# A graph network layer on one core: six of 512 gathered edge-tile pairs fetched by SyncE, and a shifted schedule

## The reference

```
ea  = edge_attr @ w_e + b_e               # 131072 x 64 by 64 x 256
msg = relu(x[src] + ea)                   # a gather of 131072 rows of x, 1 KB each
agg = segment_sum(msg, dst, 8192)
t   = x + agg
h_local = bn1(relu(t @ w1 + b1) @ w2 + b2 + x)
# attention in blocks of 32 nodes, 4 heads
q, k, v = split(x @ in_w.T + in_b)
h_attn  = bn2(softmax(q k / 8) v @ out_w.T + out_b + x)
o   = h_local + h_attn
o   = bn3(o + relu(o @ m_w1 + m_b1) @ m_w2 + m_b2)
out = layernorm(x + o)
```

## Time and profile before

| | |
|---|---|
| median of three runs | 1324.22 us (1323.06 to 1324.55) |
| the profiled execution | 1324.22 us |
| its span, first to last instruction | 1322.4 us |
| mean granted TensorE clock | 0.947 |
| instructions | 22286 |

### The profile page before, as it was taken

How to read it: one execution, slowest core, us unless ns; L and a number is a source line. 1 busy time by engine, 2 the same in 40 slices (tenths; PEclk the granted TensorE clock), 3 DMA queues, 4 the chain that set the end, 5 groups by cost and what they waited for, 6 DMA issues and landing times.

```text
span 1322.4 us, 22286 instructions
## 1 busy us (share of the span) xinstructions
PE 1174.0 (89%) x7309; PEld 664.5 (50%) x7309; DVE 823.5 (62%) x2089; ACT 548.5 (41%) x1077; POOL 971.0 (73%) x1032
## 2 busy tenths in 40 slices
PE   6787899898989898898998899889898899999987
PEld 3444454444445454454444445444454446766666
DVE  5747467667565675756667475575655757558544
ACT  1443435343434444344343434434343434444443
POOL 7777777777777777777777777777777777777760
PEclk7787999899989989899999999899898999999999
DMA  9464545555556555555555555555564555645540
GB/s 332 130 180 149 178 130 177 170 169 169 155 152 178 168 164 169 159 180 153 170 159 179 153 152 175 164 170 154 159 185 147 169 170 152 186 146 160 171 134 20
DMA packets 113268, 216.10 MB, mean 163 GB/s; under 512 B 21504, under 2 KB 62720, under 8 KB 113152
## 3 DMA queue, kind: packets, MB, share of 16 engines
q0 software_dynamic: 49152, 134.28, 34.9%
q1 hardware_dynamic: 62560, 77.09, 18.0%
q10 hardware_dynamic: 1440, 3.29, 0.6%
HBM read 197.80 MB, written 16.78 MB: 162 GB/s over the span
## 4 chain that ended last, share of the span: by engine, by line
POOL 34%; PE 27%; issue 15%; DVE 13%; DMA 5%; DVEq 4%; ACT 1%
POOL xg L369 34%; PE bank L747 16%; PE bank L777 6%; DMA xg<-in_x_dram,srcs 5%; DVE bank L592 4%; DVEq L608 3%; PE bank L792 3%; DVE mx L636 2%; DVE aggT L624 2%; DVE dif L641 2%; PE bank L801 1%; PE bank L874 1%; DVE o L668 1%; PE bank L848 1%; DVE probT L657 1%
## 5 line engine op out<-in xcount | busy, mean ns | idle before, releaser
L369 POOL DMA_INDIRECT xg<-in_x_dram,srcs x1024 | 970.1, 947 | 313.2 <-issue 301.9
L394 ACT ACTIVATE msg<-bank 128x512 f32<-128x512 f32 x512 | 277.8, 594 | 421.4 <-PE bank L777 420.9
L592 DVE TENSOR_TENSOR bank<-xg,bank 128x512 f32<-128x512 f32 x512 | 335.7, 689 | 121.1 <-DMA xg<-in_x_dram,srcs 97.6
L777 PE MATMUL bank<-we,ea 64*128 64x256 f32 x2048 | 307.1, 420 | 79.6 <-DVE bank L592 78.7
L777 PEld LDWEIGHTS bank<-we,ea 64*128 64x128 f32 x2048 | 188.1, 195 | 233.4 <-issue 188.9
L624 DVE TENSOR_TENSOR aggT<-bank,aggT 128x64 f32 x512 | 115.2, 225 | 273.2 <-PE bank L801 114.1
L792 PE MATMUL bank<-msg,onehot 128*32 128x256 f32 x2048 | 142.9, 398 | 40.6 <-DVE aggT L624 33.5
L747 PE MATMUL bank<-xT,iwT 128*128 128x512 f32 x256 | 135.9, 657 | 5.6 <-DMA xT<-in_xT_dram 5.6
L747 PE MATMUL bank<-o,m 128*128 128x512 f32 (+2 forms) x352 | 123.7, 485 | 0.4 <-DVE o L668 0.4
L747 PE MATMUL bank<-h,m 128*128 128x512 f32 (+2 forms) x352 | 116.8, 479 | 1.0 <-ACT h L454 1.0
L792 PEld LDWEIGHTS bank<-msg,onehot 128*32 128x32 f32 x2048 | 57.4, 111 | 107.0 <-issue 60.2
(11 more groups left out here) (90 smaller groups left out, 955.6 us busy)
## 6 DMA issues: line engine op xcount, KB each, us to landing
ea<-in_ea_dram SPq DMA_DIRECT2D x128, 256.0 KB
xg<-in_x_dram,srcs POOLq DMA_INDIRECT x1024
xT<-in_xT_dram SPq DMA_DIRECT2D x32, 256.0 KB, 3.9
aggT<-in_xT_dram SPq DMA_DIRECT2D x32, 256.0 KB, 3.9
oT_dram<-oT SPq DMA_DIRECT2D x32, 256.0 KB
xn<-in_x_dram SPq DMA_DIRECT2D x32, 256.0 KB
out_dram<-xn SPq DMA_DIRECT2D x30, 256.0 KB, 2.9
m<-in_m_dram ACTq DMA_DIRECT2D x2, 512.0 KB, 15.3
```

Source lines behind the costliest of these rows:

```text
L369: pool.indirect_dma_start(xg[:, q % NX, n * C:(n + 1) * C], None, t["x"], bass.IndirectOffsetOnAxis(k.srcs[:, at:at + 1], 0)).then_inc(s_x ...
L394: nc.scalar.activation(msg[:, q % NM, :], EA[q % 4][:, :], ACT.Relu).then_inc(s_msg, 1)
L592: nc.vector.tensor_tensor(EA[q % 4][:, :].rearrange("p (a c) -> p a c", a=2), xg[:, q % NX, :].rearrange("p (a c) -> p a c", a=2), KB[:, 0 ...
L777: ins = nc.tensor.matmul(EA[(2 * d + pair) % 4][:, two * C:(two + 1) * C], ea[rows, n % NEA, at:at + P], k.we[rows, :], start=False, stop= ...
```

## The change

Six of the 512 pairs are no longer gathered by POOL. Their numbers follow from `FETCHED`: 101, 181, 261, 343, 423 and 503. SP loads the numbers of their rows, eight at a time, into registers and issues one transfer of 1 KB for each of the 256 rows of a pair, into two buffers `rows` beside `xg`. The 1536 rows are spread evenly over turns 1 to 242, at the end of SP's work of a turn, and a pair is used nine turns after its last row (`OFF_LEAD`). Each pair has two semaphores of its own. POOL's buffers go by the place of a pair among the 506 others.

A group is summed in turn 2n + 1, the turn of its last messages: on PE behind attention and nodes, and on ACT the copy of it as well. One-hots are made two turns sooner. The node blocks start two turns sooner, the last of them one. DVE loads the four starts of a group's windows by one instruction, for which `base_i` holds them side by side.

```
+NOFF, ROWS, LOADED = 6, 2 * P, 8
+OFF_TURNS, OFF_LEAD = 242, 9
-FIRST_256 = {12: 213, 13: 219, 14: 225, 15: 231, 16: 237, 17: 245}
+FIRST_256 = {12: 211, 13: 217, 14: 223, 15: 229, 16: 235, 17: 243}
 NODES_128 = {
-    18: {"w1": (249,), ..., "out": (256,)},  19: {"w1": (252,), ..., "out": (259,)},
-    20: {"w1": (256,), ..., "out": (263,)},
-    21: {"w1": (257,), "B": (258,), "z": (259,), "m1": (259,), "m2": (260,), "T": (261,),
-         "log": (261,), "y": (262,), "xn": (), "out": (263,)},
+    18: {"w1": (247,), ..., "out": (254,)},  19: {"w1": (250,), ..., "out": (257,)},
+    20: {"w1": (254,), ..., "out": (261,)},
+    21: {"w1": (256,), "B": (257,), "z": (258,), "m1": (258,), "m2": (259,), "T": (260,),
+         "log": (260,), "y": (261,), "xn": (), "out": (262,)},
-SUMS = {(2 * n + 3 if n < NG - 4 else 2 * n + 2): n for n in range(NG)}
+SUMS = {2 * n + 1: n for n in range(NG)}
+def row_turn(i):
+    return 1 + i * OFF_TURNS // (NOFF * ROWS)
+FETCHED = [2 * (row_turn(ROWS * (n + 1) - 1) + OFF_LEAD) + 1 for n in range(NOFF)]
+GATHERED = [q for q in range(NP) if q not in FETCHED]
-            plan, base = NODES, 16 * b + 21
+            plan, base = NODES, 16 * b + 19
...
+            def fetch_row(i):                                        # SP
+                n, two, e = i // ROWS, i % ROWS // P, i % P
+                if i == 0:
+                    sp.wait_ge(s_of_rows, 16)
+                if i % LOADED == 0:
+                    if i % ROWS == 0 and n >= 2:
+                        sp.wait_ge(s_seed, FETCHED[n - 2] + 1)
+                    at, col = i % (P * LOADED) // LOADED, i // (P * LOADED) * LOADED
+                    _, loaded[0] = nc.values_load_multi_w_load_instructions(
+                        k.of_rows[at:at + 1, col:col + LOADED], engines=(mybir.EngineType.SP,), ...)
+                sp.dma_start(k.rows[e:e + 1, n % 2, two * C:(two + 1) * C],
+                             t["x"][bass.ds(loaded[0][i % LOADED], 1), :]).then_inc(s_row[n][two], 16)
...
+            sp.dma_start(k.of_rows[:, :], t["of_rows"]).then_inc(s_of_rows, 16)
...
+                for row in range(NOFF * ROWS):                       # end of a turn of SP
+                    if row_turn(row) == turn:
+                        fetch_row(row)
...
-            for q in range(NP):                                      # POOL
+            for slot, q in enumerate(GATHERED):
...
+                if slot >= NX and slot % 2 == 0:
+                    pool.wait_ge(s_seed, GATHERED[slot - NX + 1] + 1)
...
+                if q in FETCHED:                                     # DVE, seed
+                    n = FETCHED.index(q)
+                    pair = k.rows[:, n % 2, :]
+                    for two in range(2):
+                        dve.wait_ge(s_row[n][two], 16 * P)
...
-                at = [nc.vector.value_load(k.base_i[0:1, sub, n:n + 1], min_val=0, max_val=N - W)
-                      for sub in range(SUB)]
+                _, at = nc.values_load_multi_w_load_instructions(
+                    k.base_i[0:1, n, :], engines=(mybir.EngineType.DVE,), ...)
...
-                if turn % 2 == 1 and 1 <= turn // 2 < NG:
-                    make_onehot(turn // 2)
+                if turn % 2 == 1 and turn // 2 + 1 < NG:
+                    make_onehot(turn // 2 + 1)
...
-                if turn in SUMS:                                     # PE, behind the transposes
-                    sum_group(SUMS[turn])
                 weights(turn)
                 for J, stage, n in heads_in(turn, ("q", "k", "sc", "v", "av")):
                     attention(J, stage, n)
                 for b, stage, use in nodes_in(turn, ("T", "m2", "m1", "B", "w1")):
                     node(b, stage, use)
+                if turn in SUMS:
+                    sum_group(SUMS[turn])
```

More of the change, by code:

```diff
@@ L172, in gnn_layer @@
         k.xg = sb("xg", [P, NX, 2 * C])
+        k.rows = sb("rows", [P, 2, 2 * C])
+        k.of_rows = sb("of_rows", [P, -(-NOFF * ROWS // (P * LOADED)) * LOADED], i32)
         k.ea = sb("ea", [P, NEA, 4 * P])
@@ L220, in program @@
         s_bias, s_spread = sem("s_biases_made"), sem("s_base_copied")
+        s_of_rows = sem("s_of_rows_loaded")
+        s_row = [[sem(f"s_rows_{n}_{two}") for two in range(2)] for n in range(NOFF)]
         s_ea = [sem(f"s_edge_attr_{n}") for n in range(NEA)]
@@ L294, in preload @@
                              t["xT"][i, :, :, :]).then_inc(s_pre[i % 2], 16)
+            loaded = [()]
+            def fetch_row(i):
[7 more added lines that the diff above has]
+                    _, loaded[0] = nc.values_load_multi_w_load_instructions(
+                        k.of_rows[at:at + 1, col:col + LOADED], engines=(mybir.EngineType.SP,),
+                        min_val=0, max_val=N - 1,
+                        skip_runtime_bounds_check_because="src holds numbers of rows of x")
+                sp.dma_start(k.rows[e:e + 1, n % 2, two * C:(two + 1) * C],
+                             t["x"][bass.ds(loaded[0][i % LOADED], 1), :]
+                             ).then_inc(s_row[n][two], 16)
             sp.dma_start(k.srcs[:, 0:8 * TG], t["srcs"][:, 0:8 * TG]).then_inc(s_src, 16)
@@ L359, in _ @@
                            allow_small_or_imprecise_dtypes=True).then_inc(s_ident, 1)
-            for q in range(NP):
-                if q == 0:
+            for slot, q in enumerate(GATHERED):
+                if slot == 0:
                     pool.wait_ge(s_src, 16)
-                if q == 8 * PG:
+                if slot == 8 * PG:
                     pool.wait_ge(s_src2, 16)
-                if q >= NX and q % 2 == 0:
-                    pool.wait_ge(s_seed, q - NX + 2)
+                if slot >= NX and slot % 2 == 0:
+                    pool.wait_ge(s_seed, GATHERED[slot - NX + 1] + 1)
                 for n in range(2):
@@ L476, in _ @@
                     node(b, stage, use)
+                if turn in SUMS:
+                    copy_agg(SUMS[turn])
             with act.If(act.value_load(k.bad_i[0:1, 0:1], min_val=0, max_val=1) > 0):
@@ L532, in _ @@
             step_of(ins)
-            nc.vector.tensor_copy(k.base_i[:, :, :].rearrange("p s n -> p (s n)"),
-                                  X[:, 0:SUB * P])
+            nc.vector.tensor_copy(k.base_i[:, :, :].rearrange("p n s -> p s n"),
+                                  X[:, 0:SUB * P].rearrange("p (s n) -> p s n", n=P))
             step_of(nc.vector.tensor_reduce(k.bad[:, :], G[:, 0:P], AX.X, ALU.max))
@@ L586, in seed @@
             def seed(q):
-                dve.wait_ge(s_xg[q % NX], 32 * (q // NX + 1))
+                if q in FETCHED:
[3 more added lines that the diff above has]
+                        dve.wait_ge(s_row[n][two], 16 * P)
+                else:
+                    slot = GATHERED.index(q)
+                    pair = xg[:, slot % NX, :]
+                    dve.wait_ge(s_xg[slot % NX], 32 * (slot // NX + 1))
                 if q == 0:
@@ L593, in seed @@
                     EA[q % 4][:, :].rearrange("p (a c) -> p a c", a=2),
-                    xg[:, q % NX, :].rearrange("p (a c) -> p a c", a=2),
+                    pair.rearrange("p (a c) -> p a c", a=2),
                     KB[:, 0:C].unsqueeze(1).to_broadcast([P, 2, C]), ALU.add
@@ L607, in add_agg @@
             def add_agg(n):
-                at = [nc.vector.value_load(k.base_i[0:1, sub, n:n + 1], min_val=0, max_val=N - W)
-                      for sub in range(SUB)]
+                _, at = nc.values_load_multi_w_load_instructions(
+                    k.base_i[0:1, n, :], engines=(mybir.EngineType.DVE,), min_val=0, max_val=N - W,
+                    skip_runtime_bounds_check_because="the minimum with N - W bounds each start")
                 dve.wait_ge(s_aggT, n + 1)
@@ L723, in _ @@
                         seed(q)
+                if turn - 1 in SUMS:
+                    add_agg(SUMS[turn - 1])
                 if turn == 0:
@@ L956, in _ @@
                     transpose_agg(SUMS[turn - 1])
-                if turn in SUMS:
-                    sum_group(SUMS[turn])
                 weights(turn)
@@ L1250 @@
         "srcs": src.reshape(NG * TG, P).T,
+        "of_rows": np.concatenate([src.reshape(NP, ROWS)[q] for q in FETCHED] + [
+            np.zeros(-NOFF * ROWS % (P * LOADED), src.dtype)]).reshape(-1, P, LOADED).transpose(
+                1, 0, 2).reshape(P, -1),
         "dst_g": dst.reshape(NG, GE),
```

9 lines of the change are left out of this document (3 added, 6 removed), and 12 rows, old and new, of the table NODES_128.

## The result

The changed kernel took 1307.23 us in the median of four runs (1305.83 to 1307.93), the kernel before 1324.18 us on the same chip: 0.9872 of it, 95% interval 0.986 to 0.9885. The forecast was 1304 us, faster. The profiled run took 1307.37 us for a span of 1305.6 us.

The account below looks back on a forecast made before the run. POOL's gathers were taken to set the pace until about turn 216, then PE's order of work. 1322.4 - 12.5 - 7 = 1302.9, taken as 1302.5, plus 1.8 gave 1304 us; range 1297 to 1345, likeliest case 1297 to 1311.

Parts of the forecast that it names:

- POOL's list: Gathers on POOL until turn 216: five of the six pairs moved off it end that stretch 12.5 us sooner.
- The seeds' waits: VectorE's seeds until 1100 us stood 97.2 us for gathers, so the gain there was taken whole.
- floor for POOL: Last gather on POOL, 15.0 us sooner, starts at 1269.0 us; with landing and tail the end is at 1300.9.
- SyncE's rows: Row transfers on SyncE: 0.58 us each from transfer, gaps, address and load share; SP 88% busy, no pair late.
- The rival in which each row holds SP until it lands: On SyncE, 3.9 us a row, 6.0 ms in all; given 0.01 of the 0.20 chance of a slow SyncE.
- The limit of 0.70 us a row: On SyncE: from this cost of a row on, pairs are late and SP times the kernel; chance 0.20.
- The order's 7 us: After turn 216, sooner sums, nodes, one-hots and one load of four shrink PE's 23.2 us idle by 7.
- a tail of 26 us: From the start of the last two seeds to the end: 26 us instead of 30.4, with three stages moved ahead.
- The collision that it knew: Blocks 19 and 20 start in the turn of the add they wait for: up to 1.3 us of PE each.
- POOL's path: End of the kernel by POOL: last gather 1269.0, 0.95 to run, 4.9 to land, 26 to the end: 1300.9 us.
- The later path: End of the kernel by PE: 1322.4 - 12.5 - 7 = 1302.9 us, later than POOL's 1300.9, so it counts.
- PE takes over: Rival: PE's chains and added waits lose half the first gain or all the second: 1311 to 1320 us; chance 0.16.

Follow-up runs that it names:

- the second profile: The changed kernel run again, unedited, beside the other runs on one chip: 1304.77 us, 0.9875 of the kernel before, a span of 1303.1 us.

## Why the prediction was right, and which step was not

**POOL's list.** Right. The prediction has the first stretch end 12.5 us sooner; it was 12.9 and 13.0 in two profiles, 14.5 with rows alone and nothing with the order alone. The seeds' waits, taken as proof that the compute side could follow, were that. Its floor for POOL was 3.8 us low: the last gather was due at 1269.0 us and started at 1272.8, by 2.6 us of late seeds and about 1 us of pace (0.947 against 0.946 us each). Behind it the last seed came 1.8 us after the gather's end, where the sum had 4.9 us to land.

**SyncE's rows.** Right at 0.53 us against 0.58. Two of its terms missed against each other: the transfer was 0.23 us instead of 0.33, and address and gaps together were 0.20 instead of 0.13 (0.53 less the transfer and the load's 0.10). The load of eight was 0.80 us instead of 0.72. The rival in which each row holds SP until it lands falls with 0.53 us. The Trainium skill's Runtime: NRT & Kernel Launch (section Instruction fetch mechanics) has about 200 ns for each register, where it speaks of the runtime's own loads; the trace of this kernel's loads doesn't agree, as eight took 0.80 us and one 0.50, some 40 ns for each further one. The limit of 0.70 us a row was one of the pairs' lead; the runs with eight pairs and with single loads showed that the edge features behind the rows are late first, which the prediction named as next in line and costed at nothing: at eight pairs SP's own time, 1335.3 us less 85 us of waits, was 1250 us, too much already while every row was in time.

**The order's 7 us.** This is the step that was mis-sized, and its parts had the wrong values. It measured 3.9 us (6.3 in the second profile), and 4.3 us by itself. The prediction wanted it from PE's idle time behind turn 216, 23.2 us less 7; the idle time was 24.2 and 24.3 us, and what got less was PE's work there, by the 39 matmuls that moved ahead of turn 216. That the move itself gains is not shown: with the load of four and the old order that stretch takes 217.6 us with all its 1437 matmuls. Two errors went against each other. The prediction moved three stages ahead of the last seeds and took a tail of 26 us for it; the stages did move (158 matmuls from turn 254 on instead of 203), but from the start of the last two seeds to the end it was 32.5 us. The collision that it knew, a node block starting in the turn of the add that it needs, it held to 1.3 us of PE; it was 3.6, because the add stood behind a seed that waited for the last gather, and the clock then cost up to 2.7 us more. With that one collision taken away the tail from the same seeds is 25.4 us, though they start 2.3 us later there. The node stages two turns sooner were to gain and cost about 5 us (0.9834 against 0.9872 and 0.9875). On the other side the one load of four was priced for the last adds alone (2.83 us of wait); it is worth 6 us in the old order and 9 in the new, since the same wait stood all through the kernel before, 104.3 us in all. That the sum came within some 3 us of the measured time is therefore in part luck: by POOL's path its errors are 3.8 us on the last gather, 3.1 the other way on the landing, and 4 on the tail. (The later path, 1302.9 us, went on as 1302.5; with 1302.9 the forecast is 1304.7.)

**PE takes over** was half true: behind turn 216 PE's stalls on VectorE do block POOL, 2.6 us of it, and 2.7 us with seven pairs.

## What to carry to other kernels

When a queue that paces a kernel gets shorter, look first at how much the engines behind it stood waiting for it; here that showed that the gain could be taken whole. Work that is moved sooner must still come after what it needs on every in-order engine: an add behind a seed that waits for a gather is as late as that gather. Address loads in front of an engine's work cost on every round, not only where their wait shows on the last one.

## What the runs showed that was not expected

A stall of PE can cost twice. Behind 3.6 us without a matmul the clock showed 0.60 and 0.55 for some 8 us, and the matmuls of that time took nearly twice as long; avoiding 2.2 us of stall gave back 2.7 us of PE's busy time as well. How much differs: beside the second profile the same step gave back 1.6 us, and in that profile behind a stall of 3.7 us that ended at 1107.7 us the clock stayed at 1.00.

A load of several registers costs far less than as many loads of one: on SP 0.80 us for eight and 0.50 for one, on VectorE 0.34 us for four (median of 128 loads in the changed kernel) where one took 0.30.

SyncE issues a transfer of one 1 KB row, with the row's number from a register, in 0.23 us, less than the 0.34 of its block transfers.
